# Chunk 0's loads in another order, its units in pairs, W0 ordered by two engines, and weight groups at every 12 products

## The chip, the core and the metric

The kernel runs on one core of one Trainium2 chip. The metric is device time in microseconds of one execution. Of the kernel before there are three runs: 508.92, 509.6 and 510.27 us, median 509.6. One further execution was profiled.

## The reference

A batch of 2048 samples, each with 27 feature rows of 128 numbers (x) and one more row of 128 (x_mlp). Per sample all 351 dot products of two different feature rows are formed; with x_mlp and one zero column they make an input of 480 numbers for a four-layer MLP with ReLU, followed by one output row:

```python
dots = jnp.einsum('bfd,bgd->bfg', bottom_output, bottom_output)      # [2048, 27, 27]
pairs = dots[:, _TRIL_I, _TRIL_J]                                    # 351 pairs, i > j
x = jnp.concatenate([bottom_mlp_output, pairs, zeros(B, 1)], axis=1) # [2048, 480]
for w, b in ((w0, b0), (w1, b1), (w2, b2), (w3, b3)):                # 1024, 1024, 512, 256 rows
    x = jax.nn.relu(x @ w.T + b)
return x @ w_out.T + b_out                                           # [2048, 1]
```

All inputs are float32. The products of the MLP are made from a high and a low part of each operand: weight high x input high, weight low x input high, weight high x input low. So each 128x128 tile of a weight costs three matmuls ("products"), 408 per chunk in four layers.

## The kernel before

The batch goes in 8 chunks of 256 samples. For every chunk there are two kinds of work.

*The interaction of the chunk.* x of a chunk comes in 16 units of 16 samples (432 rows). TensorE needs each unit turned, with the 128 numbers on the partitions. In chunk 0 TensorE turns it itself: `turn_early` makes four transposes of 108 rows into PSUM, ScalarE copies them to the buffer xt (`early_copy`), TensorE forms the unit's grams, 16 small matmuls for 16 samples (`gram`), and VectorE moves them to the tile grams (`early_move`). For the later chunks SyncE loads x in blocks of 32 numbers, four loads of 64 KB a unit (`load_rows`, into the ring rows), VectorE transposes a unit in place of TensorE (`turn_raw`), and ScalarE moves the grams (`move_gram`). When a chunk's 16 units are done, grams is written to DRAM (the spill: four loads of 216 KB into blocks, `spill_quad`) and read back with the pairs on the partitions (the gather: four pieces, `gather_piece`, into the tile pairs).

*The MLP of the chunk.* TensorE runs the 408 products; ScalarE drains each finished tile with bias and ReLU (`drain`, L763), VectorE makes its high part (`split_high`), GpSimd its low part (`split_low`).

While TensorE multiplies chunk c, the units of chunk c+1 go between the products, two at each hook (every 36 products; in chunk 0, whose hooks are finer, every 30), and the first units of chunk c+2 near the end of chunk c. ScalarE may overwrite grams only when the spill of the chunk before has landed: `move_gram` of unit 0 waits for it.

All weights are transposed once by TensorE in the beginning, in 35 groups (34 of four 128x128 tiles, one of small vectors): `turn_weights`, then `weights_hi` on ScalarE and `weights_lo` on VectorE. W0's 351 pair columns must first be brought into the order in which the gather delivers the pairs: 71 copies on GpSimd (L535). W0's eight groups come before chunk 0, 7 of W1's 16 between the first products of chunk 0 and its pairs (`W1_EARLY`), the others at hooks of six products, W2's and W3's in the one bank side_ps.

The order of the work on every engine is written out by hand: `first_steps` lists what goes before chunk 0, `chunk_steps` what belongs to a chunk, with the steps at the hooks from `first_hooks` or `hooks_of`; each engine walks the same lists and picks its own steps. An engine does its instructions strictly in this order, so one that waits holds up all behind it. Almost all DMAs are issued by SyncE (SP), in the order of its own block (L419 on); ScalarE issues half of chunk 0's spill and gather. A row load into a slot of the ring waits until the unit that lay there has been transposed. SyncE's part for a chunk reads:

```python
load_mlp(c + 1)
for u in range(ROWS_RING if start else ROWS_RING + AHEAD_UNITS, UNITS):
    load_rows(c + 1, u)
...
for u in range(ROWS_RING):
    load_rows(c + 2, u)
spill(c + 1)
gather(c + 1)
```

Of the kernel before, what the change touches and what calls it, by code (L numbers as in the profile page):

```python
# [14 lines left out]
P = 128  # L15
# [12 lines left out]
ROWS_RING = 4  # L28
# [13 lines left out]
BEFORE_CHUNK, LATE_WEIGHTS = ORDER.index(W1_ALL[0]), ORDER.index(W2_ALL[0])  # L42
# [12 lines left out]
ACC_RING, GRAM_RING, TURN_RING = 3, 4, 2  # L55

XT_RING, XT_LAG, UNIT_LAG = 8, 2, 1
# [8 lines left out]
W1_EARLY, FIRST_UNIT, LATE_HOOK = 7, 6, 22  # L66
# [3 lines left out]
EARLY_SLOTS, SHORT_LAG = 8, 2  # L70
# [75 lines left out]
def first_steps():  # L146


    steps = []
    for u in range(UNITS + XT_LAG):  # L150
        if u < UNITS:
            steps.append(("turn", u))
        if 1 <= u <= SHORT_LAG:
            steps.append(("early", u - 1))
        elif u >= XT_LAG + SHORT_LAG:
            steps.append(("early", u - XT_LAG))
    steps += [("spill",), ("mlp",)] + [("weights", n) for n in range(BEFORE_CHUNK)]
    return steps + [("gather",)]


def first_hooks():


    places = [FIRST_UNIT + 5 * i for i in range(UNIT_HOOKS)]
    hooks = [[] for _ in range(3 * sum(K_TILES[n] * M_TILES[n] for n in range(3)) // FIRST_HOOK)]
    for n in range(BEFORE_CHUNK + W1_EARLY, LATE_WEIGHTS):
        hooks[n - BEFORE_CHUNK - W1_EARLY].append(("weights", n))
    for u, place in enumerate(places):
        hooks[place] += unit_steps(u, 1)
    for n in range(LATE_WEIGHTS, W_GROUPS):  # L170
        hooks[LATE_HOOK + 3 * (n - LATE_WEIGHTS)].append(("weights", n))
# [16 lines left out]
def chunk_steps(now, ahead, first):  # L188

    steps, done = [], 0
    hooks = first_hooks() if first else hooks_of(now, ahead)
    every = FIRST_HOOK if first else HOOK
    hooks.reverse()

    def products(layer, m, k, k1, parts):
        nonlocal done
        while k < k1:
            n = k1 - k  # L200
            n = max(1, min(n, (every - done % every) // len(parts)))
            steps.append(("mm", layer, m, k, k + n, parts))
            k += n
            done += len(parts) * n
            passed = done % every < len(parts) * n
            if passed and hooks:
                steps.extend(hooks.pop())
            if passed and done // every == OUT_HOOK:

                steps.append(("out",))  # L210

    if first:
        steps += [("mm", 0, m, 0, 1, ALL) for m in range(EARLY_TILES)]
        steps += [("weights", BEFORE_CHUNK + n) for n in range(W1_EARLY)] + [("pairs", 0)]
# [21 lines left out]
def dlrm_program(nc, x, x_mlp, w0, b0, w1, b1, w2, b2, w3, b3, w_out, b_out, y):  # L236
    weights = [w0, w1, w2, w3]
    biases = [b0, b1, b2, b3]
    with ExitStack() as ctx:
# [20 lines left out]
        stage_pairs, = shared(("stage_pairs", [P, 8, PAIRS + 1]))  # L260
# [23 lines left out]
        w0_pairs_loaded = sem("w0_pairs_loaded")  # L284
        w0_in_order = sem("w0_in_order")
        w0_dense_loaded = sem("w0_dense_loaded")
# [36 lines left out]
        full_dims = [[DIM, FULL_ROWS], [GROUP * step_n, UNIT_GROUPS], [1, DIM]]  # L323
# [22 lines left out]
        def turned_bank(u):  # L346

            return side_ps if u % TURN_RING else acc[:, ACC_RING - 1]
# [13 lines left out]
        def weight_bank(n):  # L362

            return gram_ps[:, n % GRAM_RING, :] if n < LATE_WEIGHTS else side_ps[:, :]
# [6 lines left out]
        def samples(u):  # L371

            return xt[:, u % XT_RING].rearrange("p j (s f) -> p j s f", s=GROUP)[:, :, :, 0:FEATS]

        def gram_found(u):

            return gram_ps[:, u % GRAM_RING, 0:P].rearrange("p (j f) -> p j f", f=QUAD)[:, :, 0:FEATS]
# [5 lines left out]
        def turned_cols(u):  # L383

            return turned_bank(u)[:, 0:UNIT_COLS].rearrange("p (j s f) -> p j s f", s=GROUP, f=FEATS)
# [10 lines left out]
        def early_rows_of(u):  # L396

            if u < EARLY_SLOTS:
                return early_rows[:, u]
            u -= EARLY_SLOTS  # L400
            return rows[:, u] if u < ROWS_RING else early_rows[:, u - ROWS_RING]

# [16 lines left out]
        def _(sp):  # L419
            def load_early(u):  # L420
                if u >= EARLY_SLOTS + ROWS_RING:

                    sp.wait_ge(turned, u - EARLY_SLOTS - ROWS_RING + 1)
                sp.dma_start(early_rows_of(u)[0:FULL_ROWS], x_full[0, u]).then_inc(early_loaded[u], 16)  # L424
# [97 lines left out]
        def _(pool):  # L522
# [9 lines left out]
            pool.wait_ge(w0_pairs_loaded, 16)  # L532
            ordered = raw_rows(0)[:, :, DIM:]
            for col, n, q, step in ROW_RUNS:
                nc.gpsimd.tensor_copy(ordered[:, :, q:q + (n - 1) * step + 1:step], stage_pairs[:, :, col:col + n])  # L535
            nc.gpsimd.tensor_copy(ordered[:, :, PAD_ROW:PAD_ROW + 1], stage_pairs[:, :, PAIRS:]).then_inc(w0_in_order, 1)
# [23 lines left out]
        def _(pe):  # L560
            def turn_weights(n):

                g, bank, ring = ORDER[n], weight_bank(n), GRAM_RING
                if n < ring:

                    pe.wait_ge(grams_done, UNITS + 1 - ring + n)
                elif ring <= n < LATE_WEIGHTS:
# [11 lines left out]
                if g < W0_GROUPS:  # L579
                    layer, m, part = 0, g, 0  # L580
                    if g == 0:
                        pe.wait_ge(w0_in_order, 1)
                        pe.wait_ge(w0_dense_loaded, 16)
                else:
                    row, part = (g - W0_GROUPS - 1) // 2, (g - W0_GROUPS - 1) % 2
                    if row < 8:
                        layer, m, loaded = 1, row, w1_loaded[row // 2]
                    elif row < 12:
                        layer, m, loaded = 2, row - 8, w2_loaded[(row - 8) // 2]
                    else:  # L590
                        layer, m, part, loaded = 3, g - W3_ALL[0], 0, w3_loaded
                    if part == 0:
                        pe.wait_ge(loaded, 16)
                src = raw_rows(layer)[:, m, :]
                for k in range(4):
                    at = (4 * part + k) * P
                    last = nc.tensor.transpose(bank[:, k * P:(k + 1) * P], src[:, at:at + P], ident[:])  # L597
# [16 lines left out]
            def gram(d, u):  # L614
# [4 lines left out]
                if isinstance(d, int) and d == 1 and u < GRAM_RING:  # L619
                    if u == 0:  # L620

                        pe.wait_ge(w_done, LATE_WEIGHTS)
                elif not (isinstance(d, int) and d == 0 and u < GRAM_RING):

                    pe.wait_ge(grams_done, d * UNITS + u + 1 - GRAM_RING)
                for j in range(UNIT_GROUPS):
                    for s in range(GROUP):
                        at = slice(QUAD * s, QUAD * (s + 1))
                        last = nc.tensor.matmul(gram_found(u)[at, j], xt[:, u % XT_RING, j, at], samples(u)[:, j, s],  # L629
# [94 lines left out]
        def _(act):  # L724
# [10 lines left out]
            def early_copy(u):  # L735
# [4 lines left out]
                nc.scalar.activation(samples(u), turned_cols(u), ACT.Copy).then_inc(xt_done, 1)  # L740

            def move_gram(d, u):
# [5 lines left out]
                nc.scalar.activation(gram_place(u), gram_found(u), ACT.Copy).then_inc(grams_done, 1)  # L748
# [76 lines left out]
        def _(dve):  # L825
# [21 lines left out]
            def early_move(u):  # L847

                dve.wait_ge(gram_done, u + 1)
                nc.vector.tensor_copy(gram_place(u), gram_found(u)).then_inc(grams_done, 1)  # L850
# [55 lines left out]
            nc.vector.memset(xt.rearrange("p r j (s f) -> p (r j s) f", f=QUAD)[:, :, FEATS:], 0.0).then_inc(xt_zeroed, 1)  # L906
            for step in first_steps():
                if step[0] == "early":
                    early_move(step[1])
                elif step[0] == "weights":  # L910
# [35 lines left out]
```

## Time and profile before

| | |
|---|---|
| median of three runs | 509.6 us (508.92 to 510.27) |
| the profiled execution | 510.51 us, its span 508.4 us |
| TensorE matmul busy | 485.8 us, 96% of the span |
| TensorE weight loads busy | 467.0 us, 92% |
| VectorE, ScalarE, GpSimd busy | 170.0, 161.6, 132.7 us |
| DMA moved | 53.88 MB, 106 GB/s in the mean; 265126 of 281091 packets under 512 B |
| chain that ended last | PE 84%, SP's queue 8%, DMA 6% |

The 2.1 us between the span and the execution's time lie outside what the profile shows. A busy share is a mean over the whole span: the stretches differ, and the page's 40 slices show TensorE at 6 to 8 tenths in the first seven and at 9 (90% or more) from then on. In the rows further below times are in us from the start of the span; "SPq" is SyncE's queue issuing a DMA, "ACTq" ScalarE's; what stands in brackets is the idle time before an instruction and what ended it; PEclk is the granted clock of TensorE, 1.00 for 2.4 GHz and 0.50 for 1.2 GHz.

### The profile page before, as it was taken

The numbers are of one execution on the slowest core, as the hardware profiler recorded it, in microseconds if no ns is written. First come the engines' busy times: TensorE is split into PE (matmuls) and PEld (weight loads), VectorE is DVE, ScalarE is ACT, GpSimd is POOL, SyncE is SP. The second block draws the span as 40 slices with busy tenths as digits, with TensorE's granted clock in tenths as the row PEclk, the third lists the DMA queues.
The fourth block names the chain that finished last, engine by engine and source line by source line (L and its number), as shares of the span: only waits on it lengthen the run. The fifth ranks groups of instructions, "written<-read, shape, count | busy, mean of one in ns | idle before, by whom it ended". The sixth has DMA issues, their size and how long they took to land.

```text
span 508.4 us, 18568 instructions
## 1 busy us (share of the span) xinstructions
PE 485.8 (96%) x7595; PEld 467.0 (92%) x7595; DVE 170.0 (33%) x384; ACT 161.6 (32%) x380; POOL 132.7 (26%) x242
## 2 busy tenths in 40 slices
PE   6687967999999999999999999999999999999998
PEld 5576967999999999999999999999999999999997
DVE  1156624444322442134322442144322533131100
ACT  3255523424322342224222332224222432233112
POOL 1530311223312242123222232223222332124221
PEclk9679999999999999999999999999999999999999
DMA  8995876756666556744665556754565564300000
GB/s 219 246 314 143 231 130 100 117 106 123 101 99 121 103 92 108 133 90 77 100 101 113 102 90 95 139 98 68 91 106 125 84 95 72 71 30 2 1 0 1
DMA packets 281091, 53.88 MB, mean 106 GB/s; under 512 B 265126, under 2 KB 279230, under 8 KB 281022
## 3 DMA queue, kind: packets, MB, share of 16 engines
q1 hardware_dynamic: 279090, 52.22, 54.2%
q8 instruction: 60, 0.98, 0.8%
q10 hardware_dynamic: 1932, 0.61, 0.5%
q14 instruction: 9, 0.07, 0.1%
HBM read 45.71 MB, written 7.09 MB: 104 GB/s over the span
## 4 chain that ended last, share of the span: by engine, by line
PE 84%; SPq 8%; DMA 6%; DVE 1%; issue 1%; ACT 0%
PE acc L671 74%; PE gram_ps L629 8%; SPq L442 6%; DMA rows<-in_r_bottom_output_dram 4%; DMA blocks<-grams 2%; SPq L424 1%; PE side_ps L602 1%; PE side_ps L597 1%; PE acc L602 1%; PE side_ps L692 0%; DVE xt L844 0%; SPq L445 0%; SPq L394 0%; PE side_ps L645 0%; PE side_ps L686 0%
## 5 line engine op out<-in xcount | busy, mean ns | idle before, releaser
L671 PE MATMUL acc<-h_a,w_hi 128*128 128x256 f32 x1152 | 221.2, 287 | 0.0
L671 PEld LDWEIGHTS acc<-h_a,w_hi 128*128 128x128 f32 x1152 | 182.9, 191 | 2.2
L763 ACT ACTIVATE h_full<-acc,small_t 128x256 f32<-128x256 f32 x175 | 83.1, 475 | 264.7 <-PE acc L671 264.1
L671 PE MATMUL acc<-h_a,w_lo 128*128 128x256 f32 x576 | 158.6, 283 | 0.0
L542 POOL TENSOR_TENSOR h_a<-h_full,h_a 128x256 fp32r<-128x256 f32 x96 | 72.2, 752 | 175.2 <-DVE h_a L856 175.2
L671 PEld LDWEIGHTS acc<-h_a,w_lo 128*128 128x128 f32 x576 | 110.4, 192 | 0.0
L671 PE MATMUL acc<-x,w_hi 128*128 128x256 f32 x504 | 97.4, 286 | 1.1 <-ACT x L773 1.0
L671 PE MATMUL acc<-h_b,w_hi 128*128 128x256 f32 x512 | 96.8, 285 | 0.0
L542 POOL TENSOR_TENSOR h_b<-h_full,h_b 128x256 fp32r<-128x256 f32 x64 | 47.2, 739 | 179.3 <-DVE h_b L856 179.3
L671 PEld LDWEIGHTS acc<-x,w_hi 128*128 128x128 f32 x504 | 80.5, 191 | 2.3 <-ACT x L773 1.8
L671 PEld LDWEIGHTS acc<-h_b,w_hi 128*128 128x128 f32 x512 | 81.3, 192 | 0.2
L844 DVE STREAM_TRANSPOSE xt<-rows 128x512 f32<-128x512 f32 x112 | 73.5, 690 | 17.1 <-DMA rows<-in_r_bottom_output_dram 16.5
L671 PE MATMUL acc<-x,w_lo 128*128 128x256 f32 x252 | 70.4, 283 | 0.0
L671 PE MATMUL acc<-h_b,w_lo 128*128 128x256 f32 x256 | 70.0, 283 | 0.0
L856 DVE CAST h_a<-h_full 128x256 fp32r<-128x256 f32 x96 | 28.1, 293 | 123.8 <-ACT h_full L763 123.3
L856 DVE CAST h_b<-h_full 128x256 fp32r<-128x256 f32 x64 | 18.6, 292 | 142.3 <-ACT h_full L763 142.3
L629 PEld LDWEIGHTS gram_ps<-xt 128*32 128x32 f32 x4096 | 43.9, 114 | 15.8 <-issue 4.7
L629 PE MATMUL gram_ps<-xt 128*32 128x27 f32 x4096 | 51.8, 199 | 4.7 <-DVE xt L844 2.5
L671 PEld LDWEIGHTS acc<-h_b,w_lo 128*128 128x128 f32 x256 | 49.1, 192 | 0.0
L671 PEld LDWEIGHTS acc<-x,w_lo 128*128 128x128 f32 x252 | 48.3, 192 | 0.0
L748 ACT ACTIVATE grams<-gram_ps 128x108 f32<-128x108 f32 x112 | 36.0, 363 | 35.9 <-PE gram_ps L629 32.3
L597 PE MATMUL gram_ps<-ident,w_raw 128*128 128x128 f32 x96 | 14.1, 282 | 3.7 <-DVE w_lo L835 2.8
(54 smaller groups left out, 178.3 us busy)
## 6 DMA issues: line engine op xcount, KB each, us to landing
rows<-in_r_bottom_output_dram SPq DMA_DIRECT2D x444, 64.0 KB, 2.1
blocks<-grams SPq DMA_DIRECT2D x30, 216.0 KB, 4.0
w_raw<-in_L_rec_w_dram SPq DMA_DIRECT2D x6, 1024.0 KB, 7.5
early_rows<-in_r_bottom_output_dram SPq DMA_DIRECT2D x12, 224.0 KB, 5.9
stage_pairs<-in_L_rec_w_dram SPq DMA_DIRECT2D x1, 1408.0 KB, 11.7
w_raw<-in_L_rec_w_dram SPq DMA_DIRECT2D x2, 512.0 KB, 8.0
mlp_rows<-r_bottom_mlp_output_dram SPq DMA_DIRECT2D x8, 128.0 KB, 2.2
pairs<-blocks SPq DMA_DIRECT2D x8, 126.0 KB
```

Of the source, the lines that this page charges most:

```text
L424: sp.dma_start(early_rows_of(u)[0:FULL_ROWS], x_full[0, u]).then_inc(early_loaded[u], 16)
L442: sp.dma_start(dst, x_blocks[q][d, u]).then_inc(rows_loaded[r], 16)
L542: nc.gpsimd.tensor_tensor(h[:, m, 1, :], h_full[:, slot % 2, :], h[:, m, 0, :].bitcast(F32), ALU.subtract).then_inc(split_done, 1)
L597: last = nc.tensor.transpose(bank[:, k * P:(k + 1) * P], src[:, at:at + P], ident[:])
L602: last = nc.tensor.transpose(turned_bank(u)[:, j * GROUP_ROWS:(j + 1) * GROUP_ROWS], src[0:GROUP_ROWS, j, :], ident[0:GROUP_ROWS, 0:GROUP_ ...
L629: last = nc.tensor.matmul(gram_found(u)[at, j], xt[:, u % XT_RING, j, at], samples(u)[:, j, s], start=True, stop=True, tile_position=(0, Q ...
L671: last = nc.tensor.matmul(acc_slot(c, slot), weight(wp, layer, m, k), in_tile(layer, k, xp), start=(k == 0 and n == 0), stop=(k == K_TILES ...
L748: nc.scalar.activation(gram_place(u), gram_found(u), ACT.Copy).then_inc(grams_done, 1)
L763: nc.scalar.activation(h_full[:, slot % 2, :], acc_slot(c, slot), ACT.Relu, bias=small_t[:, slot:slot + 1]).then_inc(drained, 1)
L844: nc.vector.transpose(xt[:, u % XT_RING].rearrange("p j n -> p (j n)"), rows[:, r].rearrange("p j n -> p (j n)")).then_inc(xt_done, 1)
L856: nc.vector.tensor_copy(h[:, m, 0, :], h_full[:, slot % 2, :]).then_inc(high_done, 1)
```

## The change

Nine things are edited, all for the beginning:
- chunk 0's x is loaded whole before anything else, and a partition gets four rows that follow each other in DRAM (2 KB in one run) in place of four rows far apart (512 B each). xt then holds a chunk-0 unit packed, and ScalarE's copy reads with a stride (`early_xt`, `turned_cols`);
- W0 comes in one load of whole rows (`stage_w0`), behind x;
- chunk 0's units go in pairs: two turned, then the grams of the two before; four PSUM banks take turned units in place of two;
- W0's pair columns are ordered by GpSimd (36 copies) and VectorE (35 copies, `order_w0`);
- ScalarE issues its part of chunk 0's gather before it starts on the weights;
- SyncE waits for chunk 0's gathered pairs to land, and only then loads W1, a quarter of it, then rows of four units of chunk 1, then the rest of W1, then four more units;
- the ring rows has 8 slots in place of 4 (`ROWS_RING`), the ring xt 4 in place of 8;
- the grams of all units after chunk 0 use two banks, and the weight groups of W1 to W3 the other two;
- these weight groups stand at every 12 products of chunk 0, W1's too.

```diff
-ROWS_RING = 4
+ROWS_RING = 8
-ACC_RING, GRAM_RING, TURN_RING = 3, 4, 2
-XT_RING, XT_LAG, UNIT_LAG = 8, 2, 1
+ACC_RING, GRAM_RING, TURN_RING, UNIT_BANKS = 3, 4, 4, 2
+XT_RING, UNIT_LAG = 4, 1
-W1_EARLY, FIRST_UNIT, LATE_HOOK = 7, 6, 22
+W1_HOOK, FIRST_UNIT = 2, 6
...
-    for u in range(UNITS + XT_LAG):
+    for u in range(0, UNITS + 2, 2):
         if u < UNITS:
-            steps.append(("turn", u))
...
+            steps += [("turn", u), ("turn", u + 1)]
+        if u:
+            steps += [("early", u - 2), ("early", u - 1)]
+    return steps + [("spill",), ("gather",), ("mlp",)] + [("weights", n) for n in range(BEFORE_CHUNK)]
...
-    for n in range(BEFORE_CHUNK + W1_EARLY, LATE_WEIGHTS):
-        hooks[n - BEFORE_CHUNK - W1_EARLY].append(("weights", n))
+    for n in range(BEFORE_CHUNK, W_GROUPS):
+        hooks[W1_HOOK + 2 * (n - BEFORE_CHUNK)].append(("weights", n))
...
-    full_dims = [[DIM, FULL_ROWS], [GROUP * step_n, UNIT_GROUPS], [1, DIM]]
+    full_dims = [[UNIT_GROUPS * DIM, FULL_ROWS], [DIM, UNIT_GROUPS], [1, DIM]]
...
-            return gram_ps[:, n % GRAM_RING, :] if n < LATE_WEIGHTS else side_ps[:, :]
+            return gram_ps[:, n % GRAM_RING if n < BEFORE_CHUNK else UNIT_BANKS + n % 2, :]
...
-            for u in range(9):
-                load_early(u)
-            sp.dma_start(stage_pairs[:, :, :], w0_rows[:, :, DIM:]).then_inc(w0_pairs_loaded, 16)
-            for u in range(9, UNITS):
+            for u in range(UNITS):
                 load_early(u)
-            sp.dma_start(raw_rows(0)[:, :, 0:DIM], w0_rows[:, :, 0:DIM]).then_inc(w0_dense_loaded, 16)
+            sp.dma_start(stage_w0[:, :, :], w0_rows).then_inc(w0_loaded, 16)
...
-            for i in range(3):
-                load_weights(1, w1, 2 * i, 2 * i + 2, w1_loaded[i])
             spill(0, (0, 1))
             gather(0, PIECES[0::2])
-            load_weights(1, w1, 6, 8, w1_loaded[3])
-            for u in range(ROWS_RING):
+            for t in range(3):
+                sp.wait_ge(gathered[t], 16 * PIECES_OF[t])
+            load_weights(1, w1, 0, 2, w1_loaded[0])
+            for u in range(ROWS_RING // 2):
+                load_rows(1, u)
+            for i in range(1, 4):
+                load_weights(1, w1, 2 * i, 2 * i + 2, w1_loaded[i])
+            for u in range(ROWS_RING // 2, ROWS_RING):
                 load_rows(1, u)
...
-                    pe.wait_ge(w_done, n)
-                    pe.wait_ge(drained, slot_count(0, ACC_RING))
+                    pe.wait_ge(w_done, n - 1)
...
-                    pe.wait_ge(grams_done, d * UNITS + u + 1 - GRAM_RING)
+                    pe.wait_ge(grams_done, d * UNITS + u + 1 - UNIT_BANKS)
...
+            def order_w0():
+                dve.wait_ge(w0_loaded, 16)
+                ordered = raw_rows(0)[:, :, DIM:]
+                for col, n, q, step in ROW_RUNS[1::2]:
+                    last = nc.vector.tensor_copy(ordered[:, :, q:q + (n - 1) * step + 1:step], stage_w0[:, :, DIM + col:DIM + col + n])
+                last.then_inc(w0_in_order, 1)
```

How the lists of instructions move is seen best on SyncE. Before, from W1's first load to the spill of chunk 1 (blocks<-grams is a spill, pairs<-blocks a gather, rows a row load of a quarter unit, w_raw a load of weights, 128x2x1024 a piece of W1 or W2):

```order
L445 DMA w_raw<-in_L_rec_w_dram 128x2x1024 x3
L389 DMA blocks<-grams 864x1x64 x2
L394 DMA pairs<-blocks 126x1x256
L394 DMA pairs<-blocks 65x1x256
L445 DMA w_raw<-in_L_rec_w_dram 128x2x1024
L442 DMA rows<-in_r_bottom_output_dram 32x16x32 x16
L445 DMA w_raw<-in_L_rec_w_dram 128x2x1024 x2
L445 DMA w_raw<-in_L_rec_w_dram 128x2x512
L463 DMA mlp_rows<-in_r_bottom_mlp_output_dram 128x2x128
L442 DMA rows<-in_r_bottom_output_dram 32x16x32 x64
L389 DMA blocks<-grams 864x1x64 x4
```

Now, on the same engine, the spill of chunk 0 stands first:

```order
L391 DMA blocks<-grams 864x1x64 x2
L396 DMA pairs<-blocks 126x1x256
L396 DMA pairs<-blocks 65x1x256
L444 DMA w_raw<-in_L_rec_w_dram 128x2x1024
L441 DMA rows<-in_r_bottom_output_dram 32x16x32 x16
L444 DMA w_raw<-in_L_rec_w_dram 128x2x1024 x3
L441 DMA rows<-in_r_bottom_output_dram 32x16x32 x16
L444 DMA w_raw<-in_L_rec_w_dram 128x2x1024 x2
L444 DMA w_raw<-in_L_rec_w_dram 128x2x512
L462 DMA mlp_rows<-in_r_bottom_mlp_output_dram 128x2x128
L441 DMA rows<-in_r_bottom_output_dram 32x16x32 x64
L391 DMA blocks<-grams 864x1x64 x4
```

Between the two spills there were 80 row loads and four loads of weights; there are 96 and seven.

On ScalarE, behind its 16 copies of chunk 0's turned units, the list before was (x<-side_ps is the mlp rows' high part, w_hi the weights', x<-pairs the pairs'):

```order
L389 DMA blocks<-grams 864x1x64 x2
L768 ACTIVATE x<-side_ps 128x256
L732 ACTIVATE w_hi<-gram_ps 128x512 x8
L730 ACTIVATE small_t<-gram_ps 128x24
L394 DMA pairs<-blocks 56x1x256
L394 DMA pairs<-blocks 104x1x256
L732 ACTIVATE w_hi<-gram_ps 128x512 x7
L773 ACTIVATE x<-pairs 128x256 x3
```

and is now:

```order
L391 DMA blocks<-grams 864x1x64 x2
L396 DMA pairs<-blocks 56x1x256
L396 DMA pairs<-blocks 104x1x256
L772 ACTIVATE x<-side_ps 128x256
L736 ACTIVATE w_hi<-gram_ps 128x512 x8
L734 ACTIVATE small_t<-gram_ps 128x24
L777 ACTIVATE x<-pairs 128x256 x3
```

The gather went ahead of the weights, and W1's first seven groups went behind the pairs.

On TensorE the first units were turned and multiplied one by one, through two banks (acc and side_ps):

```order
L602 MATMUL acc<-ident,early_rows 128x108 x4
L602 MATMUL side_ps<-ident,early_rows 128x108 x4
L629 MATMUL gram_ps<-xt 32x27 x16
L602 MATMUL acc<-ident,early_rows 128x108 x4
L629 MATMUL gram_ps<-xt 32x27 x16
```

and are now taken two at a time, through four:

```order
L602 MATMUL acc<-ident,early_rows 128x108 x12
L602 MATMUL side_ps<-ident,early_rows 128x108 x4
L633 MATMUL gram_ps<-xt 32x27 x32
L602 MATMUL acc<-ident,early_rows 128x108 x8
L633 MATMUL gram_ps<-xt 32x27 x32
```

The number of turns and grams is the same; TensorE changes between them half as often.

## Rows read from the trace of the kernel before

**Rows 1.** Windows: stretch, its length, busy us (instructions) per engine, PEclk, DMA share, GB/s.
```profile
70.00:80.00 10.00, 6.61 (x139) 6.20 (x140) 4.59 (x9) 2.70 (x6) 2.16 (x3) 1.00 0.68 106
...
110.00:160.00 50.00, 50.00 (x815) 48.66 (x815) 16.14 (x38) 15.70 (x40) 13.02 (x18) 1.00 0.62 103
```

**Rows 2.** Timeline of TensorE at chunk 1's start: start us, busy us, what, count.
```profile
117.53 0.28 PE L671 MATMUL acc<-x,w_hi 128*128 128x256 f32 x1
```

**Rows 3.** Timeline of SyncE's queue: start us, issuing us, line, what, count.
```profile
30.57 2.29 SPq L389 DMA_DIRECT2D blocks<-grams  x2
...
39.41 1.67 SPq L394 DMA_DIRECT2D pairs<-blocks  x2
...
41.62 14.37 SPq L442 DMA_DIRECT2D rows<-in_r_bottom_output_dram  x16
...
56.03 1.51 SPq L445 DMA_DIRECT2D w_raw<-in_L_rec_w_dram  x3
...
58.32 46.02 SPq L442 DMA_DIRECT2D rows<-in_r_bottom_output_dram  x64
...
104.38 3.45 SPq L389 DMA_DIRECT2D blocks<-grams  x4
...
112.21 3.02 SPq L394 DMA_DIRECT2D pairs<-blocks  x4
...
115.27 9.13 SPq L442 DMA_DIRECT2D rows<-in_r_bottom_output_dram  x16
```

**Rows 4.** Timeline of ScalarE, in the beginning and at chunk 1's start.
```profile
33.14 4.45 ACT L732 ACTIVATE w_hi<-gram_ps 128x512 fp32r<-128x512 f32 x8
...
112.27 0.55 ACT L748 ACTIVATE grams<-gram_ps 128x108 f32<-128x108 f32 x2 [3.67 <-DMA blocks<-grams]
...
117.12 0.42 ACT L773 ACTIVATE x<-pairs 128x256 fp32r<-128x256 f32 x1 [1.44 <-DMA pairs<-blocks]
```

**Rows 5.** Chain of waits from 40 us on: start us, us, what.
```profile
70.04 2.06 SPq L442
...
72.14 0.49 SPq L442
...
90.86 0.69 PE gram_ps L629 x50
...
92.45 0.44 PE side_ps L597 x4
...
92.89 2.16 PE acc L671 x18
```

**Rows 6.** DMA issues on the page: what, count, KB each, median us to landing.
```profile
rows<-in_r_bottom_output_dram SPq DMA_DIRECT2D x444, 64.0 KB, 2.1
```

**Rows 7.** Windows of half a us, columns as in rows 1.
```profile
17.50:18.00 0.50, 0.00 (x0) 0.00 (x0) 0.00 (x0) 0.00 (x0) 0.00 (x0) 0.73 1.21 226
...
31.00:31.50 0.50, 0.50 (x4) 0.50 (x3) 0.00 (x0) 0.00 (x0) 0.00 (x0) 0.62 1.13 442
```

**Rows 8.** Timeline of TensorE in chunk 0's units.
```profile
4.23 0.95 PE L602 MATMUL acc<-ident,early_rows 108*128 108x108 f32 x4 [4.23 <-DMA early_rows<-in_r_bottom_output_dram]
...
11.38 0.59 PE L602 MATMUL acc<-ident,early_rows 108*128 108x108 f32 x4
...
12.29 0.59 PE L602 MATMUL side_ps<-ident,early_rows 108*128 108x108 f32 x4
...
18.75 0.98 PE L602 MATMUL side_ps<-ident,rows 108*128 108x108 f32 x4 [2.10 <-DMA rows<-in_r_bottom_output_dram]
...
20.25 0.98 PE L602 MATMUL acc<-ident,rows 108*128 108x108 f32 x4
```

**Rows 9.** Timelines of GpSimd and VectorE before chunk 0.
```profile
18.18 11.43 POOL L535 COPY w_raw<-stage_pairs 128x8 f32<-128x8 f32 x71 [15.70 <-DMA stage_pairs<-in_L_rec_w_dram]
...
38.55 0.14 DVE L832 TENSOR_SCALAR ones<-ident 128x1 fp32r<-128x1 f32 x1
...
6.55 0.34 DVE L850 COPY grams<-gram_ps 128x108 f32<-128x108 f32 x1 [5.01 <-PE gram_ps L629]
```

More of the change, by code:

```diff
@@ L69 @@
 FULL_ROWS = 112
-EARLY_SLOTS, SHORT_LAG = 8, 2
+EARLY_SLOTS = 8
 OUT_HOOK, EARLY_TILES = 1, 4
@@ L149, in first_steps @@
     steps = []
-    for u in range(UNITS + XT_LAG):
+    for u in range(0, UNITS + 2, 2):
         if u < UNITS:
-            steps.append(("turn", u))
[L153 to L158, printed above, removed]
+            steps += [("turn", u), ("turn", u + 1)]
+        if u:
+            steps += [("early", u - 2), ("early", u - 1)]
+    return steps + [("spill",), ("gather",), ("mlp",)] + [("weights", n) for n in range(BEFORE_CHUNK)]
 def first_hooks():
@@ L213, in chunk_steps @@
         steps += [("mm", 0, m, 0, 1, ALL) for m in range(EARLY_TILES)]
-        steps += [("weights", BEFORE_CHUNK + n) for n in range(W1_EARLY)] + [("pairs", 0)]
+        steps += [("pairs", 0)]
     for layer in range(3):
@@ L346, in turned_bank @@
         def turned_bank(u):
-            return side_ps if u % TURN_RING else acc[:, ACC_RING - 1]
+            return side_ps if u % TURN_RING == ACC_RING else acc[:, u % TURN_RING]
         mlp_bank = side_ps[:, 0:CHUNK]
@@ L369, in raw_rows, with samples, early_xt, gram_found @@
             return w_raw[:, TILE0[n] * P:TILE0[n + 1] * P].rearrange("p (m k) -> p m k", k=k)
[L371 to L377, printed above, removed]
+        def samples(d, u, j, s):
+            if isinstance(d, int) and d == 0:
+                at = GROUP_ROWS * j + FEATS * s
+                return xt[:, u % XT_RING].rearrange("p j n -> p (j n)")[:, at:at + QUAD]
+            return xt[:, u % XT_RING, j, QUAD * s:QUAD * (s + 1)]
+        def early_xt(u):
+            return xt[:, u % XT_RING].rearrange("p j n -> p (j n)")[:, 0:UNIT_COLS].rearrange("p (q h) -> p q h", h=UNIT_GROUPS)
+        def gram_found(d, u):
+            bank = u % GRAM_RING if isinstance(d, int) and d == 0 else u % UNIT_BANKS
+            return gram_ps[:, bank, 0:P].rearrange("p (j f) -> p j f", f=QUAD)[:, :, 0:FEATS]
         def gram_place(u):
@@ L400, in early_rows_of @@
             u -= EARLY_SLOTS
-            return rows[:, u] if u < ROWS_RING else early_rows[:, u - ROWS_RING]
+            return rows[:, u]
         def tile_of_group(g):
@@ L530, in _ @@
                 nc.gpsimd.memset(raw_rows(0)[:, :, DIM + t * P + n:DIM + (t + 1) * P], 0.0)
[L532 removed]
+            pool.wait_ge(w0_loaded, 16)
             ordered = raw_rows(0)[:, :, DIM:]
[L534 to L536 removed]
+            for col, n, q, step in ROW_RUNS[0::2]:
+                nc.gpsimd.tensor_copy(ordered[:, :, q:q + (n - 1) * step + 1:step], stage_w0[:, :, DIM + col:DIM + col + n])
+            nc.gpsimd.tensor_copy(ordered[:, :, PAD_ROW:PAD_ROW + 1], stage_w0[:, :, DIM + PAIRS:]).then_inc(w0_in_order, 1)
             def split_low(c, layer, m):
@@ L596, in turn_weights @@
                     at = (4 * part + k) * P
-                    last = nc.tensor.transpose(bank[:, k * P:(k + 1) * P], src[:, at:at + P], ident[:])
+                    cols_k = stage_w0[:, m, 0:DIM] if layer == 0 and k == 0 else src[:, at:at + P]
+                    last = nc.tensor.transpose(bank[:, k * P:(k + 1) * P], cols_k, ident[:])
                 last.then_inc(w_turned, 1)
@@ L618, in gram @@
                     pe.wait_ge(xt_zeroed, 1)
-                if isinstance(d, int) and d == 1 and u < GRAM_RING:
+                if isinstance(d, int) and d == 0:
+                    if u >= GRAM_RING:
+                        pe.wait_ge(grams_done, u + 1 - GRAM_RING)
+                elif isinstance(d, int) and d == 1 and u < UNIT_BANKS:
                     if u == 0:
-                        pe.wait_ge(w_done, LATE_WEIGHTS)
-                elif not (isinstance(d, int) and d == 0 and u < GRAM_RING):
-                    pe.wait_ge(grams_done, d * UNITS + u + 1 - GRAM_RING)
+                        pe.wait_ge(w_done, BEFORE_CHUNK)
+                else:
+                    pe.wait_ge(grams_done, d * UNITS + u + 1 - UNIT_BANKS)
                 for j in range(UNIT_GROUPS):
                     for s in range(GROUP):
-                        at = slice(QUAD * s, QUAD * (s + 1))
-                        last = nc.tensor.matmul(gram_found(u)[at, j], xt[:, u % XT_RING, j, at], samples(u)[:, j, s],
+                        at, one = slice(QUAD * s, QUAD * (s + 1)), samples(d, u, j, s)
+                        last = nc.tensor.matmul(gram_found(d, u)[at, j], one, one[:, 0:FEATS],
                                                 start=True, stop=True, tile_position=(0, QUAD * s))
@@ L909, in _ @@
                     early_move(step[1])
+                elif step[0] == "spill":
+                    order_w0()
                 elif step[0] == "weights":
```

27 lines of the change are left out of this document (11 added, 16 removed).

## Prediction

> **What bounds the kernel now.** I read the stretches first [rows 1]. From 110 us on TensorE is busy without a gap (50.00 of 50 us at 110 to 160), and nothing of the change makes its work there smaller; the idle time lies in the first 90 us, such as 3.4 us between 70 and 80. So the change is worth what it does to the moment at which chunk 1's products run on a fully fed TensorE: the first of them that reads pairs stands at 117.53 [rows 2]. Every later chunk follows at a fixed pitch.
>
> What does that product wait for? SyncE's queue gives the answer [rows 3]: it issues the spill of chunk 0 at 30.57 and its gather at 39.41, then in one stream a piece of W1, 16 row loads, W2 and W3 (three loads in 1.51 us), the next chunk's mlp rows and 64 row loads, and only then the spill of chunk 1, at 104.38. Its gather follows at 112.21, 7.83 us after that spill began. ScalarE stands at its move of chunk 2's first gram until the spill has landed (3.67 us, to 112.27) and then for the gathered pairs (1.44 us, to 117.12) [rows 4]. The product at 117.53 comes 0.4 us behind that last step. So the chain that sets chunk 1's start is a queue: spill 0, gather 0, all loads issued up to spill 1, spill 1, gather 1. TensorE, never idle there, has a slack of some 0.3 us against it.
>
> What the queue costs per load stands in the chain of waits [rows 5]: 0.49 us for one 64 KB row load (0.53 with the gap to the next), and one in some sixteen takes 2.06. 16 loads with nothing else under way took 9.13 us, 0.57 each; the 64 behind W2 and W3 took 46.02 [rows 3], so W2 and W3 left a backlog of 46.0 - 64 x 0.57 = 9.5 us at most, or 46.0 - (64 x 0.53 + 4 x 1.4) = 6.5 us. A row load lands 2.1 us after its issue [rows 6], so it is issuing and not moving that limits.
>
> **The change part by part.**
>
> *The first units.* x comes first, in runs of 2 KB in place of 512 B. With W1's 4 KB runs under way the DMA engines moved 442 GB/s [rows 7]; near that rate a unit of 0.23 MB lands every 0.6 us, faster than TensorE takes them, so TensorE waits for nothing after its start at 4.23. At half rate a unit takes 1.50 us (18.75 to 20.25), at full rate 0.91 us (11.38 to 12.29); the full rate had begun by 11.38 and was lost in the waits for x that ended at 18.75 [rows 8]. Without these waits 4.8 units are done by 11.38, and the other 11.2 take 0.91, or 0.87 as I estimate for pairs, which change half as often between turns and grams: the grams end near 21.1 and spill 0 is issued near 21.4, not at 30.57. With no W1 in flight I give the spill 2.29 us of issuing on two queues and then the 4.38 us that lay between the end of spill 1's issuing and its gather [rows 3]: it lands at 28.1, not at 39.41. **Term A: -11.3 us.** Ends: full rate from the start and a spill of 6 us, -15; half rate throughout, 4.2 + 16 x 1.50 and on, -4.
>
> On the clock there is a rule that speaks against this term: the Trainium skill, "TensorE: Matmul & The Clock Gate", Part 4: PE-mode transpose, says that the full clock doesn't engage for transposes, which don't count as TensorE being busy in the same way. By that rule all 16 units go at half rate and term A is -4. The rows are of two minds: the first stretch of turns and grams came to full rate within 7.1 us of work, the second, from 18.75, stayed at 0.50 until past 31 [rows 7, 8]. I take the first, since the new start is the same unbroken work; the other is rival 2.
>
> *W0 by two engines.* GpSimd's 71 copies took 11.43 us; 36 of them take 5.8. VectorE's 35 cost between 0.14 (a 128x1 operation) and 0.34 us each (a move of a gram) [rows 9]: 5 to 12 us from 21, an end between 26 and 33. ScalarE can't start on the weights before its part of the gather is issued, which now stands ahead of them: 28.1 + 1.9 = 30; eight copies of W0 at 0.56 [rows 4], the mlp's and the first of pairs put chunk 0's products at 36, or up to 3 us later behind a slow VectorE. TensorE isn't what chunk 1 waits for (below), so I put this edit at 0, with -1 and +1 as ends.
>
> *W1 behind the gather.* SyncE now waits for the gathered pairs to land before it issues the first of W1. The gather's issue takes 1.67 us on SyncE and about 1.9 on ScalarE; in chunk 1 the pieces had landed some 2.3 us behind the last issue (115.23 to about 117.5). That makes 4.2 us, 2.5 of them pure waiting, and behind this wait stands every load of chunk 1. **Term B: +2.5** (ends 2 and 5). Three pieces of W1 (3 MB) that were loaded before spill 0 now stand between gather 0 and spill 1: 1.5 us of issuing, as for W2's and W3's three, and a backlog: 2.5 MB of W2 and W3 left 6.5 to 9.5 us, so 3 MB leave 7.5 to 11.4. I take the lower, from the issues counted one by one. **Term C: +9.0** (ends 1.5, if the backlog hides, and 13).
>
> *Eight row buffers.* With eight in place of four, chunk 0's part of the queue loads eight units of chunk 2 ahead of spill 1, not four: 16 more loads at 0.57. **Term D: +9.1** (ends 8.5 and 11.5). The last of them waits for VectorE's transpose of chunk 1's last unit, as before; by then that is long done.
>
> Sum: -11.3 + 2.5 + 9.0 + 9.1 = +9.3 us. Spill 1 is issued at 113.7 and lands at 121.5, and chunk 1's products start 9.3 - 0.3 = 9.0 us later, at about 126.5.
>
> *Weights every 12 products, two banks, an xt ring of four.* 16 groups of W1 cost TensorE 0.44 us each between products [rows 5], 7 of them now in the stream and no longer in the wait for pairs: 3.1 us. From 36, 372 products at 0.12, 26 groups at 0.44 and 9 pairs of units at 0.69 end at 98 with no wait. There are waits: the second piece of W1 stands behind 16 row loads, is issued 0.5 + 14.4 us behind the gather's landing, at 47, and lands at 52 or later, when TensorE wants it at 46.5; the rows of units 8 and 9, behind W2, hold it for some 5 us more. That makes 108 to 113, still ahead of 121.5, when ScalarE is let go. So the queue covers all of this; were the queue quick, it would be the bound. In the later chunks the same 64 loads stand between gather and spill, split otherwise: 0.
>
> *The clock once more.* TensorE then stands for some 9 us, where the granted clock fell to 0.50 in the waits that ended at 18.75 [rows 7, 8]. Behind that it works at half rate for a time: 7.1 us in the first stretch, over 12 in the second, half of it lost. **Term E: +3.5**, ends 0 and +6.2; no row shows dense products at half rate.
>
> Total +12.5: the profiled execution's 510.5 us (its span of 508.4 and 2.1 around it) becomes 523.0; the median of the runs stands 0.9 below, so 522.1.
>
> **The rivals.**
> 1. *The queue is not the bound: faster.* If the W loads hide behind the issuing (term C's lower end, and W2's the same) and no load takes over 0.53, then gather 0 at 28.1 + 4.2, 96 x 0.53 and 4 us for the rest put spill 1 near 87, and TensorE decides: 98 and 3 for layer 3, so chunk 1's products start at 102 to 105 in place of 117.5: 496. This decides as soon as spill 1 is issued before 104.4. For it: most issues take 0.49. Against: the long ones stand all along the queue, and the 64 loads took 46.0, not 34.
> The Trainium skill, "DMA: Bandwidth & Descriptors", Issuing engines are not separate DMA queues, says the time that a sequencer takes to initiate a DMA is usually small against the DMA itself; by that the 16 added loads would cost next to nothing, and this rival would win. The trace disagrees: 0.49 us of issue, a landing 2.1 us later with others between, and the DMA engines only 0.62 to 0.68 busy [rows 1].
> 2. *The units stay at half rate.* Term A is -4 and the rest as forecast: 522.1 + 7.3 = 529. For it: 18.75 to 31. Against: 11.38 on.
> 3. *Loss and gain cancel.* Term C at 1.5 and E at 0 leave 12.5 - 7.5 - 3.5 = +1.5; with a spill 1.5 us shorter, 509.6. The change then does what it says in chunk 0, and chunk 1 doesn't see it.
>
> **How the numbers follow.** Forecast 0.57, rival 2 0.23, rival 1 0.13, rival 3 0.07. About 0.3%, 1.5 us, is what a measurement of this kernel tells from no change. Forecast and rival 2 are slower: 0.80; rival 3 gives 0.05 to no change and 0.02 to slower; rival 1 is faster: 0.13. The forecast's own range, with C and E moved towards their ends, is 515 to 528. To hold 8 in 10 it takes in rival 2 above and rival 3 below: 508 to 532, which leaves out rival 1 and the worst of rival 2 with the upper backlog.
>
> **What would show it.** Spill 0 issued near 21 (A; at 28 it would be rival 2). SyncE idle some 2.5 us between its gather and W1 (B). 96 row loads between gather 0 and spill 1, the latter issued at 110 to 117 (C, D). ScalarE's move of chunk 2's first gram waiting 10 us or more for that spill, TensorE idle before layer 3 of chunk 0, and the granted clock at 0.50 behind that (E). From chunk 2 on the pitch of before. The forecast is wrong if spill 1 is issued before 106, or if chunk 1's products start before its gather.

## The result and the profile after

The changed kernel took 522.62 us in the median (521.59 to 523.94, 4 runs) against 509.26 us of the kernel before on the same chip: a ratio of 1.027, 95% interval 1.0235 to 1.0304. The profiled execution has a span of 522.1 us against 508.4. The forecast was 522.1 us, slower, and the path it named was the right one; but its terms have other sizes than predicted, and the largest of them failed. The profiled execution is the slowest of the four (523.94 us), and single traces of one order of loads differ by some 3 us (e9 below), so the sizes of single terms are good to two or three us.

SyncE's queue, to be laid beside [rows 3] (start us, issuing us, line, what, count):

```profile
29.94 1.39 SPq L391 DMA_DIRECT2D blocks<-grams  x2
36.55 1.65 SPq L396 DMA_DIRECT2D pairs<-blocks  x2
42.13 0.41 SPq L444 DMA_DIRECT2D w_raw<-in_L_rec_w_dram  x1
42.59 10.30 SPq L441 DMA_DIRECT2D rows<-in_r_bottom_output_dram  x16
52.93 1.51 SPq L444 DMA_DIRECT2D w_raw<-in_L_rec_w_dram  x3
54.48 16.62 SPq L441 DMA_DIRECT2D rows<-in_r_bottom_output_dram  x16
71.15 1.51 SPq L444 DMA_DIRECT2D w_raw<-in_L_rec_w_dram  x3
...
73.50 45.45 SPq L441 DMA_DIRECT2D rows<-in_r_bottom_output_dram  x64
119.00 3.59 SPq L391 DMA_DIRECT2D blocks<-grams  x4
...
125.65 3.03 SPq L396 DMA_DIRECT2D pairs<-blocks  x4
```

Spill 0 is issued hardly earlier than before (29.94, not 30.57), spill 1 is 14.6 us later (119.00, not 104.38). ScalarE's move of chunk 2's first gram waits for that spill, as in [rows 4], and then for the pairs:

```profile
125.72 0.53 ACT L752 ACTIVATE grams<-gram_ps 128x108 f32<-128x108 f32 x2 [11.67 <-DMA blocks<-grams]
128.73 0.42 ACT L777 ACTIVATE x<-pairs 128x256 fp32r<-128x256 f32 x1 [1.87 <-DMA pairs<-blocks]
```

A stand here is a time in which TensorE is idle without waiting for anything that the profile shows ("issue"). TensorE's timeline: its two stands inside chunk 0's units, the wait in front of layer 3, and chunk 1's first product of pairs, which answers to [rows 2]:

```profile
17.41 0.32 PE L633 MATMUL gram_ps<-xt 128*32 128x27 f32 x5 [2.80 <-issue]
...
23.95 0.42 PE L633 MATMUL gram_ps<-xt 128*32 128x27 f32 x25 [2.01 <-issue]
...
126.88 0.58 PE L675 MATMUL acc<-h_a,w_hi 128*128 128x256 f32 x1 [6.09 <-DVE h_a L868]
...
130.74 0.28 PE L675 MATMUL acc<-x,w_hi 128*128 128x256 f32 x1
130.86 0.28 PE L675 MATMUL acc<-x,w_lo 128*128 128x256 f32 x1
```

That product comes at 130.74 in place of 117.53, 13.2 us later; the span grew by 13.7. What follows it took 391.4 us (522.1 - 130.74), and 390.9 before. So all but 0.5 us of the loss lies ahead of it. The same sum holds in the experiments: 390.8 or 390.9 us in e1, e2 and e4 to e7, 391.5 in e9. One number of a trace, the start of chunk 1's products, tells the time of a kernel.

### The profile page after: what moved, and what is told of

The parts are those of the page before. It is cut to its first block, busy times and chain, and to the rows that moved or that the text cites. A ratio compares the mean times of both kernels' runs of the same rounds, so it can differ in the third digit from the quotient of the medians.

```text
span 522.1 us, 18558 instructions
## 1 busy us (share of the span) xinstructions
PE 487.4 (93%) x7595; PEld 470.8 (90%) x7595; DVE 172.2 (33%) x419; ACT 161.3 (31%) x380; POOL 127.1 (24%) x207
## 4 chain that ended last, share of the span: by engine, by line
PE 80%; SPq 9%; DMA 7%; issue 2%; DVE 1%; ACT 0%; ACTq 0%; DVEq 0%
PE acc L675 69%; PE gram_ps L633 8%; SPq L441 8%; DMA blocks<-grams 2%; DMA pairs<-blocks 1%; PE acc L602 1%; DMA rows<-in_r_bottom_output_dram 1%; DMA early_rows<-in_r_bottom_output_dram 1%; DMA w_raw<-in_L_rec_w_dram 1%; DVE xt L848 1%; PE gram_ps L597 1%; SPq L391 1%; PE side_ps L602 0%; SPq L396 0%; PE side_ps L696 0%
## 5 line engine op out<-in xcount | busy, mean ns | idle before, releaser
L675 PE MATMUL acc<-h_a,w_hi 128*128 128x256 f32 x1152 | 223.8, 288 | 6.9 <-DVE h_a L868 6.1
L633 PE MATMUL gram_ps<-xt 128*32 128x27 f32 x4096 | 50.4, 198 | 7.6 <-issue 4.8
L839 DVE TENSOR_TENSOR w_lo<-gram_ps,w_hi 128x512 fp32r<-128x512 f32 x34 | 23.1, 688 | 22.3 <-ACT w_hi L736 22.2
```

Source lines behind the costliest of these rows:

```text
L633: last = nc.tensor.matmul(gram_found(d, u)[at, j], one, one[:, 0:FEATS], start=True, stop=True, tile_position=(0, QUAD * s))
L675: last = nc.tensor.matmul(acc_slot(c, slot), weight(wp, layer, m, k), in_tile(layer, k, xp), start=(k == 0 and n == 0), stop=(k == K_TILES ...
L839: last = nc.vector.tensor_tensor(w_lo[:, a:b], bank, w_hi[:, a:b].bitcast(F32), ALU.subtract)
```

## The experiments

Theory: the time is set by the later of two things, the place of spill 1 in SyncE's queue or TensorE's own stream through chunk 0, and in the changed kernel it is the queue.

**e1: rows behind the gather.** Undoes the 16 added loads alone:

```diff
-                    for u in range(ROWS_RING):
+                    for u in range(ROWS_RING // 2):
                         load_rows(c + 2, u)
                 spill(c + 1)
                 gather(c + 1)
-                    for u in range(ROWS_RING, ROWS_RING + AHEAD_UNITS):
+                    for u in range(ROWS_RING // 2, ROWS_RING + AHEAD_UNITS):
```

> Undoes term D alone: 4 units of the chunk after next are loaded ahead of a spill and 8 behind its gather, where the changed kernel has 8 and 4. Queue theory: 16 fewer row loads stand between gather 0 and spill 1, so spill 1 is issued 7 to 9 us earlier than the 119.00 of the changed kernel, near 111, and chunk 1's first product of pairs moves from 130.74 to 122 to 124: about 515 us. Rival (TensorE's own stream through chunk 0, with its waits for W1, decides and the spill only ends beside it): 521 to 523 us, with spill 1 earlier all the same.

Measured: 514.82 us (ratio to the kernel before 1.012, interval 1.006 to 1.019). SyncE's queue, and TensorE at chunk 1's start:

```profile
35.71 1.66 SPq L396 DMA_DIRECT2D pairs<-blocks  x2
...
72.40 35.25 SPq L441 DMA_DIRECT2D rows<-in_r_bottom_output_dram  x48
107.70 3.42 SPq L391 DMA_DIRECT2D blocks<-grams  x4
```

```profile
121.56 0.28 PE L675 MATMUL acc<-x,w_hi 128*128 128x256 f32 x1
```

From gather 0 to spill 1 it is 71.99 us, not 82.45: the 16 loads cost 10.5 us there, more than the 7 to 9 expected. Only 9.2 us reach the products, since TensorE no longer waits in front of layer 3: now its own stream decides. The medians differ by 7.8 us, the two profiled executions by 9.8. The queue theory holds, and the changed kernel's TensorE was only some 9 us better than its queue.

**e2: W1 first again.** Three pieces of W1 ahead of spill 0, the fourth behind the gather without a wait:

```diff
+            for i in range(3):
+                load_weights(1, w1, 2 * i, 2 * i + 2, w1_loaded[i])
             spill(0, (0, 1))
             gather(0, PIECES[0::2])
-            for t in range(3):
-                sp.wait_ge(gathered[t], 16 * PIECES_OF[t])
-            load_weights(1, w1, 0, 2, w1_loaded[0])
+            load_weights(1, w1, 6, 8, w1_loaded[3])
             ...
-            for i in range(1, 4):
-                load_weights(1, w1, 2 * i, 2 * i + 2, w1_loaded[i])
```

> Undoes terms B and C alone: three pieces of W1 are loaded ahead of spill 0 and the fourth right behind gather 0, with no wait for the gather. Queue theory: the wait of 5.6 us between gather 0 and W1 goes and so does the backlog of three pieces; spill 0 itself lands up to 3 us later for the bytes beside it; spill 1 near 110 in place of 119.00 and the time near 514 us. Rival (the backlog of W1 hid beside the issuing, so only the wait goes, and the spill loses what the wait gave): 519 to 523 us.

Measured: 516.61 us (1.016, 1.010 to 1.022), between the two. The queue:

```profile
37.26 1.67 SPq L396 DMA_DIRECT2D pairs<-blocks  x2
...
39.47 24.23 SPq L441 DMA_DIRECT2D rows<-in_r_bottom_output_dram  x32
...
110.84 3.40 SPq L391 DMA_DIRECT2D blocks<-grams  x4
```

Spill 1 stands where expected, 8.2 us earlier, and chunk 1's products follow it by 11.98 us (122.82), as by 11.74 in the changed kernel. From gather 0 on 8.9 us are saved, and 0.7 lost in front of it. TensorE still waits 5.79 us before layer 3, so here the queue is the bound, with 16 loads too many. The medians differ by 6.0 us only: the profiled execution is the fastest of e2's four (515.51 us), the changed kernel's the slowest.

**e4: both undone, and all of W1 first.** e1's edit, and all four pieces of W1 ahead of spill 0, with no wait for the gather.

> All four pieces of W1 are loaded ahead of spill 0, where the DMA engines moved nearly nothing from 22 to 31 us, there is no wait for the gather, and 4 units of the chunk after next stand ahead of a spill as in the kernel before. Queue theory: spill 1 is issued at 95 to 100, ahead of what TensorE needs for chunk 0, whose products have no wait for W1 left; chunk 1's products then start near 111 by TensorE's own stream, for 501 to 506 us, less than both kernels. Rival (the spill of chunk 0 is delayed by the 4 MB in front of it by as much as is saved): about 510 us.

Measured: 508.87 us (1.001, 0.9985 to 1.0034): no difference to before. Spill 1 came at 99.69, as expected; the time did not follow, and chunk 1's products began at 116.51 with no wait in front of layer 3. I had put TensorE's stream 5 us too early. The time is near the rival's, and its mechanism is part of it: gather 0 is issued at 38.87, 2.3 us later than in the changed kernel. Where TensorE lost the time is seen in its own and in ScalarE's timeline:

```profile
29.70 1.61 PE L630 MATMUL gram_ps<-xt 128*32 128x27 f32 x108 [1.86 <-issue]
...
42.49 0.47 PE L594 MATMUL gram_ps<-ident,stage_w 128*128 128x128 f32 x1 [3.86 <-DVE w_lo L836]
```

```profile
38.88 1.91 ACTq L396 DMA_DIRECT2D pairs<-blocks  x2
40.84 0.38 ACT L769 ACTIVATE x<-side_ps 128x256 fp32r<-128x256 f32 x1 [12.68 <-issue]
41.12 2.06 ACT L733 ACTIVATE w_hi<-gram_ps 128x512 fp32r<-128x512 f32 x4
```

TensorE had filled four weight banks by 38.6, while ScalarE stood at its part of gather 0 until 40.8 and had moved none. This step came with the change (the gather stands ahead of W0's groups in the list), and under the queue it was covered.

**e6: W0's first groups ahead of the gather on ScalarE**, on top of e4:

```diff
-    return steps + [("spill",), ("gather",), ("mlp",)] + [("weights", n) for n in range(BEFORE_CHUNK)]
+    steps += [("spill",), ("mlp",)] + [("weights", n) for n in range(4)]
+    return steps + [("gather",)] + [("weights", n) for n in range(4, BEFORE_CHUNK)]
```

> The kernel of e4 with one more edit: ScalarE copies W0's first four weight groups before it issues its part of gather 0, and no longer after it. In e4 TensorE stood 3.86 us for the weight banks while ScalarE stood from 32 to 40.8 us at that gather, and chunk 0's products began at 46.32, though nothing waited for the pairs by then. Theory (since e4 TensorE's own stream decides, and a wait there now counts in full): chunk 0's products begin when the pairs land, 44 to 45 us, chunk 1's products move from 116.51 by as much, and the time is 506.5 to 507.5 us. Rival (the wait only moves to the pairs): 508.5 to 509.5 us.

Measured: 505.90 us, 0.9952 of before (0.9935 to 0.9968): half a per cent faster than the kernel before, and by more than expected. TensorE:

```profile
42.02 0.40 PE L673 MATMUL acc<-x,w_hi 128*128 128x256 f32 x1
...
112.73 0.28 PE L673 MATMUL acc<-x,w_hi 128*128 128x256 f32 x1
```

Chunk 0's products begin 4.3 us earlier than e4's 46.32, chunk 1's 3.8. I had counted on a wait for the pairs, but the first products read the mlp's part, and the pairs landed beside them.

**e9: the same edit on the changed kernel.**

> The changed kernel with the one edit of e6: ScalarE's first four groups of W0 ahead of its part of gather 0. Theory (spill 1's place in the queue sets the end, W0's work is covered): no change, 522 to 523 us, though TensorE's wait of 4.49 us for the weight banks goes and it stands the longer before layer 3. Rival (TensorE's stream through chunk 0 sets the end): 2 to 4 us faster, 518 to 520 us.

Measured: 521.48 us (1.027, 1.023 to 1.031): no change that can be told from the changed kernel's 522.62 (1.0235 to 1.0304), as long as the queue decides. The same edit is worth 3.0 us in e6. SyncE's queue and TensorE:

```profile
73.48 42.26 SPq L442 DMA_DIRECT2D rows<-in_r_bottom_output_dram  x64
115.79 3.40 SPq L392 DMA_DIRECT2D blocks<-grams  x4
```

```profile
39.52 0.39 PE L676 MATMUL acc<-x,w_hi 128*128 128x256 f32 x1
...
123.62 0.39 PE L676 MATMUL acc<-h_a,w_hi 128*128 128x256 f32 x1 [4.26 <-DVE h_a L869]
```

Chunk 0's products begin 4.5 us earlier than the changed kernel's 43.99 and gain little by it, since TensorE still waits in front of layer 3. I had expected a longer wait than the changed kernel's 6.09 us; it is 4.26, because spill 1 is issued 3.2 us earlier in this trace. The 64 loads in front of it start at 73.48, as they do there at 73.50, and take 42.26 us in place of 45.45, though no edit touches them. That is how far single traces differ.

**e7: W1 right behind the gather**, on top of e6: the four pieces issued behind the gather, still without a wait for it, and W0 divided two to one between GpSimd and VectorE.

> The kernel of e6, but W1's four pieces are issued right behind gather 0, without a wait for it to land, and GpSimd orders two thirds of W0, VectorE one third. Theory (W1 in flight delayed TensorE's instructions, with a third stall of 1.86 us behind the 468th matmul, and delayed spill 0): that stall goes, spill 0 is issued at about 29 in place of 31.74, the pairs land near 41.5, chunk 0's products begin near 42, and the time is 503 to 505 us, if spill 1 stays ahead of 104. Rival (4 MB of W1 beside the gather and ahead of 32 row loads delay the pairs or spill 1 past 106): 508 us or more.

Measured: 514.67 us (1.013, 1.010 to 1.015); the rival was right. SyncE's queue in e7, then in e6, the first row loads and spill 1:

```profile
40.13 30.29 SPq L442 DMA_DIRECT2D rows<-in_r_bottom_output_dram  x32
...
107.55 3.40 SPq L392 DMA_DIRECT2D blocks<-grams  x4
```

```profile
39.68 18.69 SPq L442 DMA_DIRECT2D rows<-in_r_bottom_output_dram  x32
...
95.91 3.86 SPq L392 DMA_DIRECT2D blocks<-grams  x4
```

32 loads take 30.29 us behind 4 MB of W1 and 18.69 without: a backlog of 11.6 us. It delays the rows that TensorE wants (5.1 us of waits for xt) as well as spill 1. The other half of the theory held: no stand behind the 468th matmul, spill 0 issued at 29.38, chunk 0's products at 39.44. Chunk 1's products (121.67) come 14.1 us behind spill 1, not 11.7 as where the queue decides, and without a wait in front of layer 3, so it is TensorE's stream with its waits that sets the end here.

**e5: chunk 0's grams twice.** Each gram matmul of chunk 0 is issued twice in a row.

> Each product of chunk 0's gram groups is issued twice in a row; the first of the two is overwritten, so the output is unchanged and TensorE has more instructions per unit. In the changed kernel TensorE stood 2.80 us behind its 219th matmul and 2.01 us behind its 343rd, each in the middle of a unit's grams. Theory that the place in the instruction stream decides (instructions arriving late): it stands again at about the 219th and 343rd matmul and then every 124 or so, which are now places in earlier units. Rival (the data or the bank of a unit decides): it stands in the same units as in the changed kernel, at higher counts. By the first theory the grams end later by more than the added products alone cost.

Measured: 535.53 us in one run. TensorE's stands inside the units:

```profile
16.78 1.06 PE L633 MATMUL gram_ps<-xt 128*32 128x27 f32 x59 [5.05 <-issue]
...
23.05 1.03 PE L633 MATMUL gram_ps<-xt 128*32 128x27 f32 x68 [2.67 <-issue]
...
30.48 0.98 PE L633 MATMUL gram_ps<-xt 128*32 128x27 f32 x88 [1.46 <-issue]
...
34.04 1.06 PE L633 MATMUL gram_ps<-xt 128*32 128x27 f32 x98 [1.32 <-issue]
...
37.63 1.43 PE L633 MATMUL gram_ps<-xt 128*32 128x27 f32 x127 [1.32 <-issue]
...
41.01 1.70 PE L633 MATMUL gram_ps<-xt 128*32 128x27 f32 x109 [1.96 <-issue]
```

Adding up the counts of TensorE's rows from the start puts these stands behind matmul 221, 348, 600, 726, 852 and 979. In the changed kernel they are behind 219 and 343. So the place in the instruction stream decides and not the unit: every 124 to 127 matmuls, with as many weight loads (behind the 474th, where one is left out, it did not stand). The page's row of DMA queues bears that out, first of the changed kernel, then of e5:

```profile
q8 instruction: 60, 0.98, 0.8%
```

```profile
q8 instruction: 64, 1.05, 0.8%
```

(packets, MB, share). 512 more matmuls and 512 more weight loads are 4 more packets of 16 KB: one packet is about 256 instructions, so about as many as lie between two stands. TensorE stands when it has used up a packet and the next is not there. The traces' DMA records show the packets themselves: in the changed kernel one moved from 14.56 to 15.76 and one from 21.33 to 22.35, and the stands end at 17.41 and 23.95. In all nine traces every such stand inside chunk 0's grams ends 1.3 to 1.7 us behind the landing of a packet.

## Why the prediction was right, point by point

*The bound.* Right: spill 1's place in the queue sets chunk 1's start. e1 and e2 move spill 1 by an edit that touches nothing else and move the time with it; e9 shows that work ahead of it is covered.

*Term A, the first units: this step failed.* Predicted -11.3 us at the gather of chunk 0, measured -2.9 (36.55 against 39.41). The spill's own part came as assumed, 6.6 us. But it was issued at 29.94, not at 21.4. Windows over chunk 0's units in the changed kernel, with columns as in [rows 1] (the last row is for term E):

```profile
4.20:14.60 10.40, 9.50 (x219) 7.86 (x220) 1.52 (x5) 4.25 (x8) 0.00 (x0) 1.00 1.02 262
...
17.40:21.00 3.60, 3.59 (x82) 3.21 (x82) 1.03 (x3) 1.06 (x2) 0.00 (x0) 0.53 1.05 395
...
24.00:27.50 3.50, 3.50 (x100) 3.13 (x100) 1.03 (x3) 1.06 (x2) 3.50 (x24) 0.53 0.02 5
...
120.00:130.00 10.00, 3.90 (x21) 3.70 (x20) 1.02 (x3) 1.56 (x5) 1.57 (x2) 0.66 0.54 121
```

The clock column needs care: the trace has no record of the clock before 13.94, and a window counts time without a record as 1.00. The pace of the instructions shows the rate there, as it did in [rows 8], where four turns took 0.98 us at half rate and 0.59 at full rate:

```profile
6.28 0.98 PE L602 MATMUL acc<-ident,early_rows 108*128 108x108 f32 x4 [0.43 <-DMA early_rows<-in_r_bottom_output_dram]
7.72 0.98 PE L602 MATMUL side_ps<-ident,early_rows 108*128 108x108 f32 x4 [0.46 <-DMA early_rows<-in_r_bottom_output_dram]
...
12.28 0.98 PE L602 MATMUL acc<-ident,early_rows 108*128 108x108 f32 x4
...
20.93 0.53 PE L602 MATMUL side_ps<-ident,rows 108*128 108x108 f32 x4
...
28.12 1.38 PE L633 MATMUL gram_ps<-xt 128*32 128x27 f32 x128
```

So the units began at half rate, and full rate came at 13.9, not at 11.38 as I had put it. It was lost again twice: behind each of the two stands the granted clock is 0.53 in the mean, near the lower of its two levels (1.2 of 2.4 GHz), for 3.6 and 3.5 us. The grams end at 29.5 (28.12 + 1.38) and not at 21.1. Of these 8.4 us the stands for instructions are 4.8 (2.80 and 2.01), two waits for x 0.9 (0.43 and 0.46), and the slower pace the remaining 2.7: TensorE's work on the units took 19.6 us, some 15.6 of them at half rate, where I had counted 16.9 with 7.15 at half rate. When the clock rises differs from trace to trace: in the experiments, which begin with the same turns, it first rose between 9.8 and 13.1.

In TensorE's timeline of the kernel before the first such stand is there too, behind matmul 218, and behind it four turns ran at full rate:

```profile
15.49 0.26 PE L629 MATMUL gram_ps<-xt 128*32 128x27 f32 x6 [2.25 <-issue]
15.68 0.59 PE L602 MATMUL acc<-ident,rows 108*128 108x108 f32 x4
```

I took it for a part of the wait for x and let it go with that. This was the first error: a wait in the middle of a unit's grams, whose data had landed, is not a wait for data. The second was the clock: I gave full rate from 11.38 on to work that I held to be unbroken. By the prediction's own mark (28 would be rival 2) spill 0 came out at rival 2, in part for its reason, the half rate, and in larger part for the stands, which no rival had.

The Trainium skill, "TensorE: Matmul & The Clock Gate", Part 4: PE-mode transpose, would have the units at half rate throughout. The trace agrees in part: some 15.6 of the 19.6 us went at half rate, all up to 13.9 among them, but turns ran at full rate too (four in 0.53 us at 20.93).

*Term B, the wait for the gather.* Predicted +2.5, measured +3.8: from the gather's issue to the first row load it is 6.04 us (42.59 - 36.55) against 2.21 [rows 3].

*Terms C and D, three pieces of W1 and 16 loads.* Predicted +18.1 together, measured +13.7: from the first row load to spill 1 it is 76.4 us against 62.8 [rows 3]. e1 gives D alone 10.5 (predicted 9.1, so 0.65 us a load), which leaves some 3 for C; e2 takes B and C away together and saves 8.9, which makes C 5.0; the two disagree by about what single traces differ. C was predicted at 9.0 (its lower bound, 6.5 us for 2.5 MB taken to 3 MB, is 7.8 and not the 7.5 that I wrote). The backlog of 3 MB is as large as I said: 16.62 + 10.30 us for 32 loads, 8.7 more than 2 x 9.13 [rows 3], and 11.6 for 4 MB in e7. But in the kernel before the 16 loads behind gather 0 already took 14.37, 5.2 more than 9.13, and that part went: behind the wait of term B they took 10.30. I had the row and did not count it. 1.5 of issuing and 8.7 of backlog less 5.2 make 5.0.

On these 16 loads the rule in the Trainium skill, "DMA: Bandwidth & Descriptors", Issuing engines are not separate DMA queues (initiating a DMA is usually short beside the DMA itself), would have given nearly nothing; e1 measured 10.5 us.

*Sum at spill 1.* -2.9 + 3.8 + 13.7 = +14.6, predicted +9.3. Spill 1 then landed 1.2 us quicker (6.65 us to its gather, 7.83 before).

*W0 by two engines, and weights every 12 products.* Put at 0, because the queue covers them; e9 shows it for the place of W0's first groups on ScalarE. The division of W0 between two engines and the 12 products were not tried by themselves. TensorE reached layer 3 at 120.8 and not at 108 to 113, mostly since its products began at 43.99 and not at 36; there was still a wait of 6.09 us. Without the cover this is the bound, as in e1 and e4.

*Term E, the clock after the wait.* Predicted +3.5, measured about 0: the half rate is there (0.66 in the mean from 120 to 130), but it lay on layer 3's products, while the pairs were still landing; chunk 1's products began at their full pitch of 0.12 us.

So the total was met (+13.7 of span against +12.5) because A's miss of +8.4 and B's of +1.3 were given back by C and D (-4.4), the quicker spill (-1.2) and E (-3.0 against the 0.5 that remain behind chunk 1's start). The chain was right; with the sizes as they came the agreement within 0.5 us is luck.

Not settled: e2, e4 and e6, in which W1 is in flight during the units, have a third stand behind matmul 468 (2.03, 1.86 and 1.77 us); where it is not, there is none in the changed kernel, e1 and e7, and one of 0.71 in e9. By the DMA records the third packet of instructions starts 5.4 to 5.5 us after the second has landed in e2, e4 and e6, and 2.8 to 3.0 in the other four, while the packet itself takes 0.9 to 1.4 us in all seven. So the packet starts later where W1 is in flight; what holds it up is not shown. Nor is it settled when a stand lets the clock fall: it did not behind the 2.25 us of the kernel before.

## What to carry to other kernels

Follow the one event from which everything behind it has a fixed length, and ask what is issued ahead of it on the same queue: 16 small loads moved ahead of a spill cost 10.5 us in that queue, and starting chunk 0's products 4.5 us earlier changed nothing that could be measured while the queue decided. A large load that is moved out of an idle time of the DMA engines into a queue takes its backlog with it (11.6 us for 4 MB). When an edit makes the bound give way, look for the next wait among those that the old bound covered: here the same move of four weight groups was worth nothing before and 3.0 us after.

## What the runs showed of the hardware

TensorE's instructions come by DMA while the kernel runs, in packets of 16 KB. In chunk 0's units, turns and small matmuls (27 columns), it used them up faster than they came, and stood for 0.71 to 5.05 us about every 125 matmuls: longest while x was loading (2.80 in the changed kernel, 5.05 in e5), 1.3 to 2.0 late in e5. The profile shows such a stand as idle time released by "issue". Behind the stands of 2.80 and 2.01 us in the changed kernel the granted clock was 0.53 for some 3.5 us; behind one of 2.25 us in the kernel before, four turns ran at full rate. The first turns and grams of a run went at half rate for 6 to 10 us, told by their pace (four turns in 0.98 us, 0.53 to 0.59 at full rate), while the clock column showed 1.00 for want of a record.
